# One norm's statistics spread over the attention, a constant moved into ScalarE's root, and the Haar attention reordered with the stream summed in PSUM

## The reference

```python
def _ln_t(v, eps=1e-05):
    m = jnp.mean(v, axis=-1, keepdims=True)
    s = jnp.var(v, axis=-1, keepdims=True)
    return (v - m) / jnp.sqrt(s + eps)

t = t + _L2_attn_ref(_ln_t(t), ...)   # norm 0: softmax attention
t = t + _L2_ffn_ref(_ln_t(t), ...)    # norm 1: 8 experts, gates per token
t = t + _L3_attn_ref(_ln_t(t), ...)   # norm 2: Haar attention
t = t + _L3_ffn_ref(_ln_t(t), ...)    # norm 3: 16 experts, top 2
```

```python
q = l2_normalize(apply_rope(x @ W_Q, cos, sin))
k = l2_normalize(apply_rope(x @ jnp.linalg.pinv(W_Q).T, cos, sin))
v = x @ W_V.T
q_coef = jnp.einsum('tw,btc->bwc', W_h, q)          # 7 Haar columns
k_coef = jnp.einsum('tw,btc->bwc', W_h, k)
attn_far = jnp.einsum('tw,bwv,sv->bts', W_h,
                      jnp.einsum('bwc,bvc->bwv', q_coef, k_coef) * scale, W_h)
attn = jnp.where(near_mask, attn_scores, attn_far)  # causal; near = own token
attn = variance_scaled_softmax(attn / jnp.sqrt(n_visible))
y = jnp.einsum('bts,bsc->btc', attn, v) @ W_O.T
```

## Time and profile before

| | us |
|---|---|
| median of 3 runs | 377.82 |
| lowest, highest | 376.14, 377.91 |
| the profiled run, its own time | 377.71 |
| its span in the profile | 375.9 |
| convolutions and norm 0, 0 to 46 us | 46 |
| softmax attention, 46 to 187 us | 141 |
| norm 1 and 8 experts, 187 to 233 us | 46 |
| norm 2 and Haar attention, 233 to 272 us | 39 |
| norm 3 and 16 experts, 272 to 376 us | 104 |

### The profile page before, as it was taken

How to read it: one execution, slowest core, us unless ns; L and a number is a source line. 1 busy time by engine, 2 the same in 40 slices (tenths; PEclk the granted TensorE clock), 3 DMA queues, 4 the chain that set the end, 5 groups by cost and what they waited for, 6 DMA issues and landing times. The chain is left out here.

```text
span 375.9 us, 6837 instructions
## 1 busy us (share of the span) xinstructions
PE 331.7 (88%) x2271; PEld 215.0 (57%) x2277; DVE 266.0 (71%) x681; ACT 220.0 (59%) x557; POOL 164.8 (44%) x176
## 2 busy tenths in 40 slices
PE   8885269999999999999798999768288999999996
PEld 5752146777787777766454333434075866666761
DVE  2888877888888888787383785795986844455551
ACT  2455358889898888988529563432225644444550
POOL 6000056655655555555300000130200699999994
PEclk9997568999999999999999999968689999999999
DMA  7953000000000000000000991000001967665521
GB/s 208 234 147 119 0 0 3 1 3 1 2 0 3 3 0 2 2 2 0 2 3 14 352 379 46 2 1 0 0 2 22 339 218 223 223 225 161 200 88 57
DMA packets 16274, 30.85 MB, mean 82 GB/s; under 512 B 5808, under 2 KB 9584, under 8 KB 16240
## 3 DMA queue, kind: packets, MB, share of 16 engines
q1 hardware_dynamic: 15776, 29.60, 24.7%
q10 hardware_dynamic: 464, 0.82, 0.9%
HBM read 29.70 MB, written 0.72 MB: 81 GB/s over the span
## 5 line engine op out<-in xcount | busy, mean ns | idle before, releaser
L531 POOL TENSOR_TENSOR va_vb<-va_vb,rowinv 128x512 f32<-128x512 f32 x64 | 66.5, 1039 | 56.3 <-DVE rowinv L1702 56.2
L667 ACT ACTIVATE va_vb<-ps,negmax 128x256 f32<-128x256 f32 x128 | 59.5, 469 | 9.8 <-DVE negmax L1695 8.9
L802 ACT ACTIVATE wy<-ps 128x512 f32<-128x512 f32 x64 | 38.1, 597 | 42.8 <-PE ps L1137 42.7
L1137 PE MATMUL ps<-XP,early 64*128 64x256 f32 x512 | 57.5, 379 | 0.0
L1137 PEld LDWEIGHTS ps<-XP,early 64*128 64x128 f32 x512 | 46.8, 186 | 12.5 <-issue 4.9
L938 PE MATMUL ps<-keys_gates,XX 128*128 128x512 f32 x128 | 47.7, 455 | 2.9 <-ACT va_vb L667 1.5
L1695 DVE TENSOR_REDUCE negmax<-ps 128x2 f32<-128x512 f32 x64 | 44.1, 689 | 1.4 <-PE ps L938 0.4
L950 PE MATMUL ps<-consts,va_vb 128*128 128x128 f32 x256 | 39.8, 279 | 4.3 <-POOL va_vb L531 3.1
L950 PEld LDWEIGHTS ps<-consts,va_vb 128*128 128x128 f32 x256 | 30.0, 147 | 12.4 <-POOL va_vb L531 6.2
L968 PE MATMUL ps<-pT,vproj 128*64 128x256 f32 x256 | 35.7, 388 | 0.0
L658 ACT ACTIVATE keys_gates<-ps 64x256 fp32r<-64x256 f32 x64 | 24.2, 378 | 9.0 <-PE ps L916 7.9
(11 more groups left out here) (322 smaller groups left out, 637.1 us busy)
## 6 DMA issues: line engine op xcount, KB each, us to landing
pT<-gates_row SPq DMA_DIRECT2D x16, 512.0 KB, 4.9
vproj<-gates_row SPq DMA_DIRECT2D x14, 512.0 KB, 5.1
gate_row_keys<-gates_row SPq DMA_DIRECT2D x14, 512.0 KB, 5.3
early<-in_f_in SPq DMA_DIRECT2D x1, 2048.0 KB, 8.2
consts<-in_consts SPq DMA_DIRECT2D x1, 813.0 KB, 9.0
x<-in_x SPq DMA_DIRECT2D x1, 512.0 KB, 3.7
w2raw<-in_f_in SPq DMA_DIRECT2D x1, 512.0 KB, 5.7
out<-in_f_out SPq DMA_DIRECT2D x1, 512.0 KB
```

The source lines that it names most:

```text
L531: gp.tensor_tensor(prob[:, n % 4], prob[:, n % 4], rowinv[:, n % 4, :].unsqueeze(2).broadcast_to([P, U, N]), ALU.mult).then_inc(S("p_scale ...
L667: ins = act.activation(prob[:, n % 4, h, :], ps[:, 1 + n % 2, h * N:(h + 1) * N], ACT.Exp, bias=negmax[:, n % 4, h:h + 1], accum_out=rowsu ...
L802: act.activation(act_out[:, kk % 2, :].rearrange("p (o n) -> p o n", o=2), ps[:, 2 * pair_of(kk):2 * pair_of(kk) + 2, 0:2 * P], ACT.Silu). ...
L1137: mm = pe.matmul(ps[:, 2 * pair_of(kk) + o, w * 2 * P:(w + 1) * 2 * P], w3raw[r, e, w * HID:(w + 1) * HID], pairs(c, 2)[r], start=True, st ...
```

## The change

There are four parts.

1. Norm 1's statistics: `bn_stats` of an image's two tiles now follows that image's `add_out`, seven images within the attention and one at its end; `layer_norm(1)` takes none. The `keep_clock` products ahead of `ln_pe(pe, 1)` go from 12 to 3.
2. In all four norms ScalarE's root takes the scale 1/64 and the constant eps (a new tile, set by GpSimd), and VectorE's operation L1641 is gone.
3. In the Haar attention the basis is made in two halves, each after its half of the rotation; TensorE waits for each half apart, and the 8 `keep_clock` products ahead of L1201 are gone. One of VectorE's softmax operations is gone: the variance is the sum of (share x score) x (score - mean).
4. The stream is put into PSUM by an identity product, and the far product is added to it there. VectorE then adds the other parts in two halves, GpSimd makes its product in two halves, and TensorE gets 8 `keep_clock` products before `haar_added` and 14 ahead of `ln_pe(pe, 3)`.

```diff
@@ l3_pool @@
-            gp.tensor_tensor(m_d[:].rearrange("p (t c) -> p t c", c=C), V3[:],
-                             pdia[:].unsqueeze(2).broadcast_to([P, TILES, C]),
-                             ALU.mult).then_inc(S("diag_done"), 1)
+            for u in range(U):
+                gp.tensor_tensor(m_d[:].rearrange("p (j u g c) -> p u j g c", j=J, u=U, g=G)[:, u],
+                                 V3[:].rearrange("p (j u g) c -> p u j g c", j=J, u=U)[:, u],
+                                 pdia[:].rearrange("p (j u g) -> p u j g", j=J, u=U)[:, u].unsqueeze(3).broadcast_to(
+                                     [P, J, G, C]), ALU.mult).then_inc(S("diag_done"), 1)
@@ gpsimd @@
+            gp.memset(eps[:], EPS_LN).then_inc(S("b2_zeroed"), 1)
@@ ln_act @@
             act.wait_ge(S("ln_var"), n + 1)
-            act.activation(lnc[:, 6, :], lnc[:, 5, :], ACT.Sqrt).then_inc(S("ln_std"), 1)
+            if n == 0:
+                act.wait_ge(S("b2_zeroed"), 2)
+            act.activation(lnc[:, 6, :], lnc[:, 4, :], ACT.Sqrt, bias=eps[:, 0:1],
+                           scale=1.0 / C).then_inc(S("ln_std"), 1)
@@ l3_pe @@
-            keep_clock(pe, 5, 8)
-            pe.wait_ge(S("rotated"), 4)
-            pe.wait_ge(S("basis_ready"), 2)
             for j in range(J):
+                if j % 2 == 0:
+                    pe.wait_ge(S("rotated"), j + 2)
+                    pe.wait_ge(S("basis_ready"), j + 2)
...
             mm.then_inc(S("far_ready"), 1)
+            for u in range(U):
+                pe.matmul(ps[:, u, :], ident, T[:].rearrange("p (j u g) c -> p u j (g c)", j=J, u=U)[:, u],
+                          start=True, stop=False, skip_group_check=True)
...
-                mm = pe.matmul(ps[:, u, :], p8T[h, :], vsum[h].rearrange("p b c -> p (b c)"), start=True, stop=True)
+                mm = pe.matmul(ps[:, u, :], p8T[h, :], vsum[h].rearrange("p b c -> p (b c)"), start=False, stop=True,
+                               skip_group_check=True)
             mm.then_inc(S("yfar_ready"), 1)
+            keep_clock(pe, 2, 8)
@@ tensor @@
             start_sums(pe, parity_chunk)
-            keep_clock(pe, 2, 12)
+            keep_clock(pe, 2, 3)
             ln_pe(pe, 1)
...
             start_sums(pe, plain_chunk)
+            keep_clock(pe, 2, 14)
             ln_pe(pe, 3)
@@ l3_vector @@
+            def basis_of(half):
+                inv = n2[:, 0, :].rearrange("p (j u g h) -> p j u (g h)", j=J, u=U, g=G)
+                j = slice(2 * half, 2 * half + 2)
+                for u in range(U):
...
             rotate(0)
-            rotate(1)
             dve.wait_ge(S("norm_ready"), 1)
             step(ts(n2[:, 2, :], n2[:, 1, :], EPS_L2, None, ALU.add))
             step(dve.reciprocal(n2[:, 0, :], n2[:, 2, :]))
...
+            basis_of(0)
+            rotate(1)
+            basis_of(1)
...
-            step(tt(t9[:], z9[:], z9[:], ALU.mult))
-            step(tt(t9[:], t9[:], table("share"), ALU.mult))
+            step(tt(t9[:], t9[:], z9[:], ALU.mult))
...
-            step(tt(t, t, m_a[:], ALU.add))
-            dve.wait_ge(S("yfar_ready"), 1)
-            tu = T[:].rearrange("p (j u g) c -> p j u g c", j=J, u=U)
             for u in range(U):
-                ins = tt(tu[:, :, u], tu[:, :, u], ps[:, u, :].rearrange("p (j g c) -> p j g c", j=J, g=G), ALU.add)
-            step(ins)
-            dve.wait_ge(S("diag_done"), 1)
-            tt(t, t, m_d[:], ALU.add).then_inc(S("haar_added"), U)
+                dve.wait_ge(S("diag_done"), u + 1)
+                step(tt(by_tiles(m_a[:])[:, u], by_tiles(m_a[:])[:, u], by_tiles(m_d[:])[:, u], ALU.add))
+                dve.wait_ge(S("yfar_ready"), 1)
+                tt(by_tiles(t)[:, u], by_tiles(m_a[:])[:, u], ps[:, u, :].rearrange("p (j g c) -> p j g c", j=J, g=G),
+                   ALU.add).then_inc(S("haar_added"), 1)
@@ layer_norm @@
-                for q in range(TILES):
-                    if n % 2 == 0 and q % 8 == 0:
-                        dve.wait_ge(S("T_act"), n + q // 8 + 1)
-                    ins = dve.bn_stats(ln6[:, q, :], T[:, q, :])
-                step(ins)
+                if n != 1:
+                    for q in range(TILES):
...
-                step(stt(lnc[:, 4, :], lnc[:, 3, :], C / 4.0, lnc[:, 2, :], ALU.mult, ALU.add))
-                ts(lnc[:, 5, :], lnc[:, 4, :], 1.0 / C, EPS_LN, ALU.mult, ALU.add).then_inc(S("ln_var"), 1)
+                stt(lnc[:, 4, :], lnc[:, 3, :], C / 4.0, lnc[:, 2, :], ALU.mult, ALU.add).then_inc(S("ln_var"), 1)
@@ add_out @@
+                dve.wait_ge(S("stream_added"), m + 1)
+                for u in range(U):
+                    q = 4 * (m // 2) + 2 * u + m % 2
+                    ins = dve.bn_stats(ln6[:, q, :], T[:, q, :])
+                if m == IMAGES - 1:
+                    step(ins)
```

17 lines of the change are left out of this document (11 added, 6 removed).

## The result

| | before | after |
|---|---|---|
| median, us | 377.53 (11 runs, 376.11 to 379.02) | 372.67 (11 runs, 371.79 to 376.23) |
| ratio | 1 | 0.9869, 95% interval 0.9845 to 0.9894 |
| the profiled execution's own time | 377.71 (span 375.9) | 376.23 (span 374.4) |

The changed kernel is 4.9 us faster; 372.7 was forecast. The profiled execution after is the slowest of its eleven, and its first part shows why. "Start" ends at the attention's first row maximum, and contains the loads of the inputs. Each number is a difference of two start times in the timeline; the last stage runs to the end of the last copy on VectorE.

The account below looks back on a forecast made before the run. The prediction saw one serial stream of tokens through norms and attentions, with TensorE or VectorE setting the pace by turns. From 377.71 us its terms summed to -5.0, giving 372.7 us; own range 371.5 to 374.0, with rivals 370.8 to 375.2.

Parts of the forecast that it names:

- Constant in the root: All four norms: dropping L1641 and its wait saves 0.21 us each in norms 0, 1 and 2; ScalarE's root costs nothing.
- Norm 1, -1.9: Norm 1: VectorE ready 1.97 us earlier, TensorE with three products meets it; gain 1.9 us, bounds 1.5 to 2.0.
- low-clock rival for norm 3: Norm 3: clock low when the sums start, rising some 4 us later; +2.1 us, 374.8 us; chance 20%.
- Seven adds, +0.5: Attention: statistics behind seven adds cost 0.1 us in each of five Newton steps; +0.5 us, bounds 0 and 2.6.
- The first part as a whole: Statistics moved from norm 1 into the attention: norm 1's -1.9 us together with the seven adds' +0.5 us.
- Unread products, -1.8: Haar attention up to the scores: the 8 removed products were all on the path; -1.8 us.
- In front of `p8`: Haar attention: identity and prefix products at the low clock make `p8` wait 0.6 us, with `yfar` and the prefix still covered.
- 3 us in hand: TensorE's margin around the identity and prefix products ahead of `p8`, should they run at the high clock.
- Softmax, -0.34: Haar attention's softmax: one VectorE operation less, 0.31 us long, 0.34 us with its wait.
- End of the Haar attention, -1.0: Last additions: the first half addition is held until GpSimd ends, about 1.4 us long; gain 1.0 us, bounds 0 and 1.8.
- Norm 3, -0.1: Norm 3: sums at the high clock and 14 products leave TensorE last by 0.07 us; gain 0.1 us.
- the rival in which the attentions give nothing: Attentions: the removed waits were hidden, so the change does nothing there; 375.5 us; chance 4%.

Follow-up runs that it names:

- e1: Changed kernel with all sixteen statistics back in norm 1 and 12 unread products ahead of its turning: 372.74 us, ratio 0.9864.
- e8: Changed kernel with each image's two statistics moved to later steps, one in each, behind the copies others wait for: 372.44 us, ratio 0.9860.
- e12: e10 with the 8 unread products put back between the Haar block sums and the scores' products: 372.33 us, ratio 0.9856.
- e9: Changed kernel with ten unread products added in the attention's last steps and ahead of norm 1's sums: 372.31 us, ratio 0.9873.
- e10: Changed kernel with the edits of e4, e8 and e9 joined: 370.37 us, ratio 0.9808.
- e2: Changed kernel with 12 unread products instead of 3 ahead of norm 1's turning: 373.91 us, ratio 0.9910.
- e6: Changed kernel without the 8 unread products behind the far product `yfar`: 374.70 us, ratio 0.9929.
- e5: Changed kernel with GpSimd's product of the diagonal as one operation instead of two halves: 372.74 us, ratio 0.9877.
- e4: Changed kernel with the last four additions reordered, the two that read PSUM first: 371.56 us, ratio 0.9856.
- e7: Changed kernel without the 14 unread products behind norm 3's sums: 374.31 us, ratio 0.9929.
- e3: Changed kernel with the 8 unread products put back between the Haar block sums and the projection on the basis: 376.22 us, ratio 0.9951.

## Why the prediction came out right, step by step

- **The total** was right to 0.1 us. As a sum of terms this is partly luck: norm 1 gave 0.5 to 0.7 us instead of 1.9 in four of the seven profiles with three products and nothing added in front, and the stretch up to the Haar scores gave 2.7 instead of 1.8 in six of the eleven profiles with this code (17.26 us, against 19.96 in the one profile of the kernel before).
- **Constant in the root.** Right: -0.19 in norm 2, -0.22 in norm 0, the same step in the others. ScalarE's root grew from 0.22 to 0.31 us beside 1.29 us of subtraction and cost nothing.
- **Norm 1, -1.9.** VectorE's part came as worked out (3.37 us to the tokens, from 5.31). The step that failed is "they start some 0.37 us later ..., run the same 2.13 us until the unread products": I gave the sums the high clock because the row before had it. In four of the eight profiles without extra work in front the clock fell there, the sums took 2.8 to 3.6 us, and the term was -0.5 to -0.7; where it held, with three products, the term was -1.93. TensorE waits 0.82 us ahead of the sums instead of 0.41, but it does so in both groups, and the nine products that are gone stood behind the sums, so neither is shown to be the cause. `e1` and the kernel before, with 0.41, held: two profiles. I had a low-clock rival for norm 3 and none for norm 1.
- **Seven adds, +0.5.** Mis-sized: +0.83. The lateness of the reciprocal was right (0.2 us), but I let the pipeline absorb half of it, by ScalarE's 0.24 us of wait. It absorbed none: five Newton adds at nearly 0.2 us each. `e8` shows that the cost lies in where and how the statistics stand, not in their number: spread over two steps, behind the copies, they cost nothing.
- **The first part as a whole**, the two terms above: forecast -1.4, by `e1` nothing that the median can tell.
- **Unread products, -1.8.** The mechanism was right: they cost 1.96 us by `e12`, 1.8 by its ratio. The stage gained 2.26 in the profile after and up to 3.7 in others, because where the clock rises within the first 8 products and the block sums differs from execution to execution: the four block sums took 1.88 (`e9`), 2.40 (`e10`), 2.91 (after) and 3.14 us (`e8`) for the same work. I had this only as a bound, "the gain is up to 1 us larger". In the profile after, the stretch from the block sums to the scores is only 1.27 us shorter (1.82 of products gone, 0.1 lost in the block sums and 0.45 to a low clock at L1219). The other 0.99 lies ahead of the block sums, in the 8 unread products that both kernels have: they took 2.40 us after, and seven of them alone 2.99 before, where the clock was still low. The kernel before has its own such spread there, so what of the extra gain belongs to the change can't be told from single profiles.
- **In front of `p8`.** Right in that nothing was late; the low clock there reached only to 263.7 us, so TensorE had 0.41 us in hand and not -0.6. What I called "3 us in hand" at the high clock is not a plain gain: `e2`, `e6` and `e10` had it (2.87 us), and in all three the clock fell behind it.
- **Softmax, -0.34**: -0.35.
- **End of the Haar attention, -1.0**: -0.97, and the 1.40 us of the first half addition as written. `e5` and `e4` confirm the cause: the addition takes 0.69 us alone, and with the PSUM additions first 0.84 us more are gained. The Trainium skill's rule that such a VectorE instruction and a GpSimd one exclude each other ("SBUF — State Buffer", "Who interferes with whom") agrees with both; by a view of sharing `e5` should have lost 0.5 us or more and lost 0.12.
- **Norm 3, -0.1**: +0.18, and -0.18 behind it. The clock held as forecast up to the end of the sums in the profile after and in nine more of the twelve that have the 8 products. In the other two, `e2` and `e10`, it fell ahead of the sums all the same, so "the work that should hold it" is only partly borne out. Without the 8 the run is 2 us longer (`e6`), without the 14 it is 1.6 (`e7`). The sums took 2.57 us at clock 1.00, not the 2.13 that I took from norm 1, so TensorE was last by 0.4 and not by 0.07.
- **Two slips.** The low clock is the first of the rivals, not "the second rival below"; and the rival in which the attentions give nothing adds up to -2.4 by the terms, 375.3 us and not 375.5. Neither bears on the forecast.

## What to carry to other kernels

When VectorE's part of a short phase shrinks, price TensorE's part at both clock levels, also where the trace before shows the high one: here the same three products took 0.8 or 1.46 us, and a gain of 1.9 on VectorE became 0.5 to 0.7 in four profiles of seven. Work that is moved into a full pipeline is best put behind what the other engines wait for: here that was the difference between 0.8 us and nothing. Products that end early leave TensorE idle: in the four profiles where it then waited 2.9 to 3.4 us, the clock fell right behind. An addition of two SBUF operands on VectorE goes after GpSimd's work, and the one with a PSUM operand beside it.

## What the runs showed of the hardware that I had not expected

- The granted clock changes its place between programs that have the same instructions there. In the profiles with nothing added ahead of norm 1 it fell there four times of eight, with the same waits in front to 0.02 us. Under or ahead of the eight products behind `yfar` it fell in the three profiles in which TensorE had waited 2.86 or 2.87 us for `p`, and in none of the ten with 0 to 1.68 us. The Trainium skill ("TensorE: Matmul & The Clock Gate", Part 1) says that the moment differs from run to run; these profiles show it, with 1.2 to 1.4 us in norm 1 and up to 2.7 us ahead of the scores.
- VectorE's addition of 512 columns from SBUF: 0.69 us, and 1.40 beside GpSimd's product of the same size; with one operand in PSUM 0.64 to 0.69 us either way.
- Norm 1's and norm 3's 32 sums are of one shape, at clock 1.00, and took 1.97 and 2.57 us. They differ in the order in which they write their columns and in what the other engines do beside them. Whether that is the cause was not tried.
- From the first instruction to the first row maximum the same code took 51.2 to 54.4 us: more than most terms of this study. In the profile after, a later transfer of `x` (1.67 us) and a low clock right behind it (0.94) make up the difference, and the execution is the slowest of its kernel; in `e3` it was a wait of 1.42 us for another input, `wqT`, with a low clock from 14 to 21 us behind it.
